# Second attention of a gated decoder: turns of normed tiles two units on, weight splits spread, the bias ahead of the reciprocals, and 128 rows in the value products

## The reference, cut to what matters

```
q = split_heads(layernorm(x) @ Wq + bq)      # 16 heads of 16
k = split_heads(ctx @ Wq + bq)               # ctx: 77 rows a batch
v = split_heads(ctx @ Wq + bq)
attn = softmax(q @ k.T / 4)                  # over 77 keys
x = x + tanh(g_xattn[1]) * (merge_heads(attn @ v) @ Wo + bo)
xn = layernorm(x)
x = x + tanh(g_ffn[1]) * ((silu(xn @ wg.T) * (xn @ wu.T)) @ wd.T)   # wg, wu, wd: int32 / 127
```

## Time and profile before

| | |
|---|---|
| median of 3 runs | 687.71 us (686.56 to 687.75) |
| the profiled execution | 686.08 us, of which the span is 684.2 us |
| second attention, 484.4 to 568.6 us of the span | 84.2 us |
| mean granted TensorE clock over the span | 0.96 |

### The profile page before, as it was taken

How to read it: one execution, slowest core, us unless ns; L and a number is a source line. 1 busy time by engine, 2 the same in 40 slices (tenths; PEclk the granted TensorE clock), 3 DMA queues, 4 the chain that set the end, 5 groups by cost and what they waited for, 6 DMA issues and landing times.

```text
span 684.2 us, 10256 instructions
## 1 busy us (share of the span) xinstructions
PE 621.6 (91%) x3676; PEld 479.4 (70%) x3676; DVE 369.2 (54%) x817; ACT 370.0 (54%) x631; POOL 142.6 (21%) x212
## 2 busy tenths in 40 slices
PE   2699888898799999999999999999789889999996
PEld 2575555554478888888887787778577767888885
DVE  6677667779573524335456435443477655343332
ACT  4316757566775746556657445446746564243232
POOL 9633265354640000000000000001245222000000
PEclk9769999999999999999999999999978699999999
DMA  7320120112130030300312430000343000000000
GB/s 229 97 77 21 32 60 11 46 49 97 31 122 4 0 124 0 123 2 0 124 32 62 94 123 2 2 0 2 94 140 94 3 2 1 1 31 1 32 31 32
DMA packets 21970, 34.68 MB, mean 51 GB/s; under 512 B 4640, under 2 KB 13216, under 8 KB 21920
## 3 DMA queue, kind: packets, MB, share of 16 engines
q1 hardware_dynamic: 19648, 30.51, 14.3%
q0 software_dynamic: 1984, 3.44, 2.2%
q10 hardware_dynamic: 288, 0.07, 0.0%
HBM read 18.93 MB, written 2.10 MB: 31 GB/s over the span
## 4 chain that ended last, share of the span: by engine, by line
PE 76%; DVE 8%; POOL 6%; ACT 6%; issue 3%; DMA 0%; DVEq 0%; ACTq 0%; POOLq 0%
PE SC L1167 28%; PE PV L1167 26%; PE PV L1187 5%; PE AUX L1167 4%; PE SC L1302 4%; PE AUX L1274 3%; ACT XN L760 2%; DVE NM L1051 2%; DVE O L1059 2%; PE AUX L1230 2%; PE PV L1274 1%; POOL RSTD L630 1%; DVE ST L969 1%; ACT PB L815 1%; POOL QG L659 1%
## 5 line engine op out<-in xcount | busy, mean ns | idle before, releaser
L911 DVE TENSOR_TENSOR HL<-HF,HH 128x512 fp32r<-128x512 f32 x120 | 83.7, 698 | 154.1 <-ACT HH L857 153.8
L815 ACT ACTIVATE PB<-SC 77x1024 f32<-77x1024 f32 x96 | 94.3, 1014 | 46.5 <-PE SC L1302 46.2
L857 ACT ACTIVATE HH<-PV 128x512 fp32r<-128x512 f32 x96 | 57.3, 597 | 66.8 <-PE SC L1167 66.8
L852 ACT ACTIVATE HF<-PV 128x512 f32<-128x512 f32 x96 | 57.3, 597 | 54.8 <-PE PV L1167 53.0
L630 POOL TENSOR_TENSOR RSTD<-RSTD,NHALF 128x4 f32<-128x4 f32 x16 | 17.4, 1089 | 321.8 <-DVE RSTD L982 321.7
L1167 PE MATMUL PV<-XH,WAH 128*128 128x512 f32 x192 | 77.7, 404 | 1.0 <-DVE O L1059 1.0
L1167 PE MATMUL SC<-HH,WBH 128*128 128x512 f32 x192 | 76.3, 397 | 0.0
L1167 PE MATMUL SC<-HH,WBL 128*128 128x512 f32 x192 | 75.7, 394 | 0.0
L1167 PE MATMUL PV<-XL,WAH 128*128 128x512 f32 x192 | 75.4, 393 | 0.0
L1167 PE MATMUL PV<-XH,WAL 128*128 128x512 f32 x192 | 75.3, 392 | 0.0
L1167 PE MATMUL SC<-HL,WBH 128*128 128x512 f32 x192 | 74.9, 390 | 0.0
(11 more groups left out here) (241 smaller groups left out, 1214.8 us busy)
## 6 DMA issues: line engine op xcount, KB each, us to landing
QG<-QH SPq DMA_DIRECT2D x96, 64.0 KB, 2.0
WSA<-in_wa SPq DMA_DIRECT2D x6, 1024.0 KB, 5.1
WSB<-in_wb SPq DMA_DIRECT2D x12, 512.0 KB, 7.0
QG<-QL SPq DMA_DIRECT2D x48, 64.0 KB, 2.0
X<-in_x SPq DMA_DIRECT2D x4, 512.0 KB, 6.0
QG<-QH POOLq DMA_DIRECT2D x32, 64.0 KB, 2.3
out_x<-X SPq DMA_DIRECT2D x4, 512.0 KB, 2.6
QG<-QL POOLq DMA_DIRECT2D x16, 64.0 KB, 2.2
```

The lines of the kernel that those rows point to most:

```text
L815: act.activation(probs(n)[0:S, :, :], SC[0:S, n % 2, :, :], ACT.Exp, scale=SCALE[a]).then_inc(exp_done, 1)
L852: act.activation(HF[s % 2][:, :], PV[:, s % 2, :], ACT.Gelu_apprx_tanh)
L857: act.activation(HH[s % 2][:, :], PV[:, s % 2, :], ACT.Gelu_apprx_tanh).then_inc(act_done, 1)
L911: return dve.tensor_tensor(dst, raw, hi.bitcast(F32), ALU.subtract)
```

## The change

1. `plan()`, tile 0: the two first weight loads are hung behind unit 0 instead of 5, and the third behind unit 5 instead of unit 4 of tile 1. The scale of ATT1 tile 3 goes from unit 2 to 3, its turn from 4 to 5.
2. The six weight splits go from tile 1 (four, at units 1, 3, 6, 7) and tile 2 (two, at units 1, 3) to tile 0 (three, at 3, 5, 7), tile 1 (one, at 2) and tile 3 (two, at 2 and 4).
3. The turns of FFN1 tiles 0 and 1 are hung three units behind their scale instead of one.
4. POOL adds the bias as soon as it comes to the step, with a wait for the norm that reads X, and waits for the reciprocals only behind it.
5. The value products read all 128 rows of PB and V in both attentions. So that the rows from 64 on are zero, POOL sets them anew at the end of the zones: two buffers once the low parts are done, and the halves of the two others behind the last two zone steps. The first exponentials wait for this (`pb_set`) instead of for the zone products.

```diff
--- before.py
+++ after.py
@@ -214,34 +214,30 @@
         side, fillers = {}, []
         if j == 0:
             side.setdefault(0, []).extend(norm(ATT1, 3))
-            side.setdefault(5, []).extend([("ffn_load", 0), ("ffn_load", 1)])
-            side.setdefault(2, []).append(("scale", ATT1, 3))
-            side.setdefault(4, []).append(("turn", ATT1, 3))
-            side.setdefault(3, []).append(("q_move", 1, 2, 0))
-            side.setdefault(7, []).append(("q_move", 1, 2, 1))
+            side.setdefault(0, []).extend([("ffn_load", 0), ("ffn_load", 1)])
+            side.setdefault(3, []).extend([("scale", ATT1, 3), ("q_move", 1, 2, 0), ("ffn_split", 0, 0)])
+            side.setdefault(5, []).extend([("turn", ATT1, 3), ("ffn_split", 0, 1), ("ffn_load", 2)])
+            side.setdefault(7, []).extend([("q_move", 1, 2, 1), ("ffn_split", 1, 0)])
         if j == 1:
-            side.setdefault(1, []).append(("ffn_split", 0, 0))
-            side.setdefault(3, []).append(("ffn_split", 0, 1))
-            side.setdefault(4, []).append(("ffn_load", 2))
+            side.setdefault(2, []).append(("ffn_split", 1, 1))
             side.setdefault(5, []).append(("query", 1, 3))
-            side.setdefault(6, []).extend([("q_move", 1, 3, 0), ("ffn_split", 1, 0)])
-            side.setdefault(7, []).append(("ffn_split", 1, 1))
+            side.setdefault(6, []).append(("q_move", 1, 3, 0))
             fillers += [(maxima(1, 2, 0), 0, 3), (maxima(1, 2, 1), 4, 7)]
             side.setdefault(4, []).append(("negmax", 1, 2, 0))
             side.setdefault(7, []).append(("negmax", 1, 2, 1))
         if j == 2:
             side.setdefault(0, []).append(("q_move", 1, 3, 1))
-            side.setdefault(1, []).append(("ffn_split", 2, 0))
-            side.setdefault(3, []).append(("ffn_split", 2, 1))
             fillers += [(maxima(1, 3, 0), 1, 5), (maxima(1, 3, 1), 5, 8)]
             side.setdefault(5, []).append(("negmax", 1, 3, 0))
         if j == 3:
             side.setdefault(0, []).append(("negmax", 1, 3, 1))
+            side.setdefault(2, []).append(("ffn_split", 2, 0))
+            side.setdefault(4, []).append(("ffn_split", 2, 1))
         if j:
             side.setdefault(5, []).append(("turn_mix", j - 1))
             side.setdefault(7, []).append(("project", j - 1))
         if j > 1:
-            norm_in(side, 0, FFN1, j - 2, 1, 1)
+            norm_in(side, 0, FFN1, j - 2, 1, 3)
         steps += attention_tile(1, j, side, fillers, left)
     steps += attention_end(left)
     steps += norm(FFN1, 2)
@@ -673,6 +669,16 @@
                     for buffer in PB + PB2[0]:
                         pool.memset(buffer[64:P, :, :], 0.0).then_inc(pb_set, 1)
                     pool.wait_ge(pb_set, 4)
+                elif kind == "zone_end":
+                    pool.wait_ge(rstd_ready, sum(NORMS.index(s) < NORMS.index(("norm", ATT1, 3)) for s in NORMS))
+                    pool.wait_ge(hl_ready, ZSTEPS)
+                    pool.memset(PB2[1][1][64:P, :, :], 0.0).then_inc(pb_set, 1)
+                    pool.memset(PB2[1][0][64:P, :, :], 0.0).then_inc(pb_set, 1)
+                    for s in range(2):
+                        pool.wait_ge(y_done, ZSTEPS - 1 + s)
+                        pool.memset(PB[0][64:P, s, :], 0.0).then_inc(pb_set, 1)
+                        pool.memset(PB[1][64:P, s, :], 0.0).then_inc(pb_set, 1)
+                    pool.wait_ge(pb_set, 10)
                 elif kind == "mix":
 
                     _, a, j, o = step
@@ -680,19 +686,21 @@
                     part = O[n % 2]
                     rz = RZ[:, n % 2, :, :]
                     xj = X[:, TT * j:TT * (j + 1), :]
-                    pool.wait_ge(rz_ready, n + 1)
                     if a == 1:
                         if o == 0:
+                            pool.wait_ge(xn_ready, order["norm", ATT1, j] + 1)
                             pool.tensor_tensor(xj, xj, BOG[:, :].unsqueeze(1).to_broadcast([P, TT, D]),
                                                ALU.add).then_inc(pool_step, 1)
                             chain += 1
                             if j:
                                 filled(pool, ("turn_mix", j - 1, KC - 1))
                         pool.wait_ge(pool_step, chain)
+                        pool.wait_ge(rz_ready, n + 1)
                         pool.tensor_tensor(MIX[:, :, P * o:P * (o + 1)].rearrange("p t (h d) -> p h t d", d=DV),
                                            part[:, :, :, 0:DV], rz.unsqueeze(3).to_broadcast([P, 8, TT, DV]),
                                            ALU.mult).then_inc(mixed, 1)
                         continue
+                    pool.wait_ge(rz_ready, n + 1)
                     pool.tensor_tensor(rz, rz, CF[:, 0:8].unsqueeze(2).to_broadcast([P, 8, TT]), ALU.mult).then_inc(pool_step, 1)
                     chain += 1
                     pool.wait_ge(pool_step, chain)
@@ -811,7 +819,7 @@
                     if n >= 4:
                         act.wait_ge(pv_done, (n - 4) // 2 + 1)
                     if a == 1 and n < A0_UNITS + 4:
-                        act.wait_ge(y_done, ZSTEPS)
+                        act.wait_ge(pb_set, (9, 10, 10, 10)[n - A0_UNITS])
                     act.activation(probs(n)[0:S, :, :], SC[0:S, n % 2, :, :], ACT.Exp, scale=SCALE[a]).then_inc(exp_done, 1)
                 elif kind == "wo_split":
                     act.wait_ge(wo_in, 32)
@@ -1175,13 +1183,12 @@
                     pe.wait_ge(pv_set, 1)
                 if q >= 1:
                     pe.wait_ge(pv_out, q)
-                rows = slice(0, P) if a == 0 else slice(0, S)
                 for i in range(2):
-                    p = probs(2 * q + i)[rows, :, :].rearrange("s i (t q r) -> s i t q r", t=TT, r=32)
+                    p = probs(2 * q + i)[:, :, :].rearrange("s i (t q r) -> s i t q r", t=TT, r=32)
                     for n in range(1 if a == 0 else 2):
                         heads = slice(0, 2) if a == 0 else slice(n, n + 1)
                         at_v = (j // 2 * (D // DV) + (2 * k + i if a == 0 else 4 * k + 2 * i + n)) * (DV + 1)
-                        v = VALL[a][rows, at_v:at_v + 32]
+                        v = VALL[a][:, at_v:at_v + 32]
                         at_h = P * (2 * i + n)
                         for r in range(4):
                             ins = pe.matmul(PV[32 * r:32 * r + 32, 0, at_h:at_h + P * (heads.stop - heads.start)], v,
```

## The result

| | before | after |
|---|---|---|
| median, same chip | 686.56 us (684.04 to 689.21, 9 runs) | 683.44 us (680.54 to 684.79, 9 runs) |
| ratio, 95% interval | | 0.995 [0.9927, 0.9973] |
| the profiled execution, its span | 686.08, 684.2 us | 683.44, 681.6 us |
| mean granted clock | 0.96 | 0.97 |

A forecast was written before the change was run, and what follows sets the result against it. TensorE, busy 91% of the span, was taken to bound the kernel through waits and lower-clock stretches; 7.5 + 0 - 0.3 + 3.8 = 11.0 us won gave 675.1 for the profiled execution, 676.7 for a median, range 669 to 685.

The forecast's parts named there:

- the 3.8 of the rows: Second attention, tile 1: value products on 128 rows shorten or prevent the 10.3 us stretch at the lower clock; 3.8 us won.
- signs named as wrong: Cold stretches of 10 us and more with 128 rows; tile 3 under 17 or over 21 us; tile 0's exponentials over 2 us later.
- 7.5 forecast: Tile 2: turn two units on and split moved away remove both waits and keep the clock up; 7.5 us won.
- 1.3 us of wait: Tile 2: TensorE wait expected to remain, as the next exponential still stands behind the scaling; about 1.3 us.
- 17.2: Tile 2: TensorE's work if all of it ran at the full clock, 17.2 us within the 26.2 us taken.
- won 2.7, lost 1.8 + 0.85: zero: Tile 3: later turn wins its 2.7 us wait; norm behind splits loses 1.8, second ScalarE split 0.85; zero in sum.
- 2 lost if the clock falls: Tile 3: lower bound on the zero, 2 us lost if the clock falls in the new wait.
- 0.3 lost: Tile 0 and start of tile 1: query tile 2's second-half maxima start near 505.5 instead of 505.18; 0.3 us lost.
- 3.3 us forecast to 495.4: Tile 0: first VectorE weight split, stretched by the bias beside it, takes 0.96 + 2.38 = 3.3 us, ending at 495.4.
- "slower" rival: Tile 0: split ending beyond about 497 holds the transpose, TensorE idles, clock falls near 496; 694.6 or 691.0 us; chance 0.06.
- 2.1 to 3.4 us to land: Tile 1: landing time assumed for SyncE's six query DMAs issued behind the third weight's load.
- 505.5: Tile 1: time near which the first maxima of query tile 2's second half start, in place of 505.18.

The follow-up runs named there:

- e4: Changed kernel with the turns of the feed-forward's normed tiles one unit behind their scaling again, as before the change: 686.58 us, ratio to before 1.0011.
- e3: Changed kernel with both splits of the third weight in tile 2 again (units 1 and 3), none in tile 3: 683.63 us, ratio to before 0.9953.
- e8: e7 with both splits of the third weight moved from tile 3 to the last unit of tile 2: 675.73 us, ratio to before 0.9844.
- e1: Changed kernel with POOL adding the bias behind the reciprocals again: 681.62 us, ratio to before 0.9928.
- e7: Changed kernel with the bias of tiles 0 and 1 added during the zones, where POOL is idle: 677.62 us, ratio to before 0.9877.
- e5: Kernel before with the bias edit alone (bias added ahead of the reciprocals): 686.74 us, ratio to before 1.0009.
- e11: e8 with both splits of the second weight at the last unit of tile 1: 676.65 us, ratio to before 0.9881.
- e6: Kernel before with the 128 rows and the memsets on POOL alone: 682.14 us, ratio to before 0.9945.
- e2: Changed kernel with the second attention's value products on 77 rows again, memsets kept: 685.72 us, ratio to before 0.9998.
- e9: e8 with the second attention's value products on 77 rows: 680.36 us, ratio to before 0.9906.
- e12: e8 with the turn of tile 3 one unit later, at unit 7 behind the projection: 674.28 us, ratio to before 0.9836.

## Why the prediction was right in sign and wrong in size

The sum was 7.5 + 0 - 0.3 + 3.8 = 11.0. By tile it should have been: tile 2 7.5 won, tile 3 nothing, tiles 0 and 1 3.5 won. The profiled executions have 6.8 won, 3.8 lost, and 0.8 lost, 2.2 in all. Three terms failed: the zero of tile 3, the 0.3 of tile 0, and the 3.8 of the rows, which hung on a stretch that gave way to a longer one behind a new wait. Of the 8.8 between 11.0 and 2.2, tile 2 has 0.7, tile 3 3.8, and tiles 0 and 1 with the rows 4.3. Of the signs named as wrong, two came: stretches of over 10 us at the lower clock with 128 rows, and a tile 3 over 21 us.

- **Tile 2: right.** 7.5 forecast, 6.8 measured; under 20 us and clock at 1.00 as said. The turn at 536.69 waits 0.20. e4 shows that the gap does it and e3 that the split's leaving is the other half; either undone, the tile takes 23 us. I kept 1.3 us of wait; there are 19.45 - 18.30 = 1.15. The work is 18.30, though, where I had 17.2: my estimate of the work at full clock, with half of the busy time at the lower clock in it, was 1.1 too low.
- **Tile 3: the step "won 2.7, lost 1.8 + 0.85: zero" failed.** Its first half held: the scaling is 1.54 us later in the tile (1.8 forecast). What I costed at 0.85, the second ScalarE split, was more: it and its VectorE half stand ahead of the high and low parts that free AUX, and TensorE waits 2.06 us at the turn for that bank. I had followed the exponentials behind the split and not the banks. Idle grew by 1.8 (2.96 to 4.76), the clock stayed down for 6.8 us in place of 3.4, busy time grew by 2.0. My bound "2 lost if the clock falls" was half of what came. e3 and e8, with the splits elsewhere, have 17.6 and idle 2.4: the splits cost 5.4 us. They do not divide it between the first split, ahead of the norm, and the second, ahead of the bank. "Won 2.7" was too much as well: even without splits the later turn trades the wait of 2.68 for two of 1.20 and 0.89, and tile 3 wins 1.7 in all (19.23 to 17.57 in e8).
- **Tile 0: the step "0.3 lost" failed, though its mechanism was right.** Split and bias meet: 3.3 us forecast to 495.4, measured 3.67 to 495.05. e1 and e7 show the cause: 0.96 without the bias beside it. The Trainium skill, "SBUF — State Buffer", section "Who interferes with whom", would have had the split, which issued first, take 0.96 and the bias wait; the trace differs, as at the earlier trace rows, and the measurement decides. But I followed that delay only along VectorE, SyncE and the DMAs to 505, and gave the transpose held behind the split to the "slower" rival, with the condition that the split end beyond 497. It ended at 495.05, and TensorE idled 1.86 us all the same: the bound was drawn too late by 2 us. So that rival's mechanism came true at a chance of 0.06, with its clock fall at 495. That the sign held is in part luck: what tile 2 won outweighed it.
- **The query DMAs: a term mis-sized.** I took 2.1 to 3.4 us to land, from DMAs issued 3 us and more behind a weight load. Just behind the third weight's load SyncE's take 5.9 in after and 5.6 in e1, and POOL's 5.6 and 5.4. In e1 the maxima start at 505.56, where I forecast 505.5, but that is luck: the DMAs are issued earlier (the last at 499.84) and land later than I thought. In after TensorE is late itself and waits for none.
- **Who held the maxima before: right.** e5 takes POOL's delay away, and the wait of 1.93 us is gone. That SyncE's DMAs would hold them next came true in e1 and e11, not in after, where they start at 509.26.
- **128 rows: right that they matter, wrong where.** I set 3.8 us on the stretch of tile 1. In after that stretch became one of 13.7 us from 495 on, since a wait of its own precedes it. On before's plan the rows give 4.0 us (e6), in after 2.3 by the medians and 3.3 by the ratios (e2), in e8 4.3 to 4.6 (e9). Their price is nothing, as forecast: a value step takes 1.08 us at full clock with 77 rows and with 128. The Trainium skill, "TensorE: Matmul & The Clock Gate", section "Part 1: The HAM clock gate", ties the gate to how busy TensorE is and says nothing of rows. By that alone 77 rows in place of 128 would make no difference to e8, and the trace does not agree with it: in e9 TensorE is busy for 16.9 us and stays at 0.50.
- **The memsets cost nothing: right.** The first exponential starts 0.80 us after the tile's first score product, 0.79 before.

How the rows come to matter to the clock is not shown. In the second attention nearly the same products follow the same waits in before and in e6, and the clock falls in one and not in the other; after has 128 rows too and stays down for 13.7 us, as long as e2 with 77 behind the same wait of 1.86 us. In e7, e8, e12 and e9 the same two waits of 0.93 and 1.13 us open tile 1; the clock is then down for 0, 3.4 and 6.8 us with 128 rows, and for 17.1 with 77. So chance has a share in a single execution. What shows that the rows matter is that three pairs, of 5 to 18 executions a kernel, differ clear of their intervals: before and e6, after and e2, e8 and e9. The last two pairs differ in the rows alone, but did not run in the same turns and are compared by their ratios to before; e6 did, and has the memsets on POOL besides.

## What to carry to other kernels

A weight split on VectorE is costed with what POOL does beside it, and then followed to every bank and buffer that the instructions behind it set free, before it is moved; the place for it is where TensorE has a long run of products that need none of them (e8). A POOL instruction whose inputs are ready early can go a whole stage earlier, to where POOL is idle (e7). Where TensorE is busy and its clock low, try products on all 128 rows, filled up with zeros: they cost nothing here and gave 2 to 5 us.

## What the runs showed of the hardware

- Much the same waits (1.4 to 2.7 us) brought 27 us at the lower clock with 77 rows in the value products and 6.8 with 128, in one execution each (before and e6); at the median of all, some 52 and 38 us of the span. That was half expected; that busy TensorE stays at 0.50 for 16.9 us (e9) was not.
- When a VectorE split and a POOL product run side by side, either may grow: split 3.67 and bias 2.38 in after, split 1.39 and bias 3.07 in e5. I had expected only the one that began first to grow.
- DMAs of 64 KB issued just behind one of 768 KB land in 5.9 us against 3.1 from SyncE, which issued the large one too, and in 5.6 against 2.1 from POOL, which did not (after and before).
